# A convolution stage on TensorE: taps for 64 rows and two heads in the two halves of the array

## The chip, the cores and the metric

The kernel runs on one core of a Trainium2 chip. The metric is the device time of one execution in microseconds (us). TensorE (PE, matmuls; PEld, its weight loads), VectorE (DVE), ScalarE (ACT), GpSimd (POOL) and SyncE (SP) each have an instruction queue of their own, and 16 DMA engines serve the DMA queue that SyncE issues to. They meet at semaphores.

## The reference

The input x is 64 batches x 32 heads x 512 positions. Two layers follow each other:

```python
# layer 0: a causal convolution per head, masked by each batch's length
kernel = 2 * real(einsum(Cs, exp(dtA * arange(512))))     # 32 heads x 512 taps
y = irfft(rfft(x * mask, 1024) * rfft(kernel, 1024))[..., :512] + x * mask * D
x = x + y * mask
# layer 1: a gated MLP with one low-rank adapter per batch
gate, up = lora(x @ W_gate.T), lora(x @ W_up.T)           # 1376 wide
x = x + lora((silu(gate) * up) @ W_down.T)
```

All is fp32. The convolution is done as matrix products: for head h, output block k (128 positions) is the sum over d of T_d times input block k-d, where T_d is a 128x128 Toeplitz matrix with the taps 128(d-1)+1 to 128(d+1)-1 in it. D and the residual are added to tap 0.

## The kernel before, in words

**Preparation (0 to 27 us).** VectorE and ScalarE build, for each of four groups of 8 heads, tables from which TensorE makes the taps (`taps`, L965, 8 small matmuls a group). VectorE copies them out of PSUM (L733, L734) and SyncE stores them to a DRAM tensor `kpad`, one row of 128 zeros and 512 taps per head (`store_taps`, L247, semaphore `k_out[group]`).

**Convolution (27 to 78 us).** The 32 heads go in 16 pairs, `PAIRS`. For each pair SyncE loads

- `um` (L258, 256 KB): the pair's input, 128 positions on the partitions, 4 blocks x 64 batches x 2 heads. The positions within a block are reversed, so that the shifted rows below make a Toeplitz matrix;
- `toep` (L253, 512 KB): the shifted taps. Partition r gets, for both heads, 512 taps beginning at r+1 of the padded row, straight from `kpad`. Columns dP to (d+1)P of it are T_d.

Both have `RC` = 4 slots, and the loads of pair p wait until pair p-4 is multiplied (`conv_ps`). TensorE's `conv(pair)` (L969 to L980) waits for the slot's two semaphores and for `x1_ok`, that the PSUM bank has been read. Then for each of the two heads and each d of 0 to 3 it makes one matmul of 128 rows, 128 weight columns and (4-d) x 64 moving columns, all into one PSUM bank: head 0 in its first 256 columns, head 1 in the others. That is 8 matmuls a pair; every fp32 matmul stands in the trace as two records, each with a weight load (LDWEIGHTS), so 16 and 16. Four banks take turns (`ps_c` = `ps_g[0]`, `ps_g[1]`, `ps_u[0]`, `ps_u[1]`). VectorE's `add_conv` (L761) puts the result into `x` where the length mask is set; the last pair is done in two pieces (`select_conv`, L769).

TensorE's order is written out by hand:

```python
taps(0); conv(0); taps(1); conv(1); conv(2); taps(2); conv(3); taps(3)
for pair in range(RC, PAIRS): conv(pair)
```

SyncE's order, too: one in-order queue for all transfers. Before and among the convolution's loads stand the loads of `x` (8 x 512 KB), the gate and up weights (`w_raw`, 12 pieces), and for the first tile of the next stage the adapter tables `a_raw` (4 x 152 KB, after pair 8's taps) and `b_raw` (L311, 4 x 64 KB, each into 16 partitions, after pair 9's). After pair 15's taps come the down weights (`wd_raw`, L236, 6 pieces) and `bd_raw`. `store_taps(2)` and `store_taps(3)` stand behind the taps of pairs 6 and 7; pair 8's taps wait for the landing of the third store.

Beside it ScalarE and GpSimd, and late in the stage VectorE, split the weights into a high and a low part (L440, L404, L776).

**MLP (79 to 543 us).** 16 tiles of 4 batches x 32 heads. For each tile TensorE multiplies x by the gate and up weights (L1024), adds the adapters, and, after the gate, multiplies by the down weights (L1062). The change touches nothing here but how the PSUM tensors `ps_g`, `ps_u` and `ps_x` are declared.

## Time and profile before

| | |
|---|---|
| median of 3 runs | 544.09 us (543.97 to 545.04) |
| the profiled execution | 544.7 us, its span 543.0 |
| mean granted clock of TensorE | 0.997 of 2.4 GHz |
| TensorE busy | 505.7 us (93% of the span), weight loads 459.8 |
| VectorE, ScalarE, GpSimd busy | 344.3, 190.5, 41.5 us |
| chain that ended last | PE 86%, DVE 6%, DMA 5% |
| HBM | 52.89 MB read, 8.47 MB written |

The rows speak of two stages: TensorE is the bound in the MLP stage, and the transfers share the convolution stage with it. In a row, `L978` is the line of the kernel, `ps_g<-um,toep` what is written and read, `128*128` rows and columns of the weights, and `[2.30 <-DMA toep<-kpad]` the idle time before the group and what ended it. A group's duration is from its first start to its last modelled end, so it is longer than the distance to the next group.

### The profile page before, as it was taken

The page shows a single profiled execution, that of the slowest core. Times are in us where ns is not written, and L with a number is a line of the kernel's source. Part 1 is how long each engine was busy: PE and PEld are TensorE (multiplying, and loading weights), DVE is VectorE, ACT ScalarE, POOL GpSimd, SP SyncE. Part 2 cuts the span into 40 slices and gives each one's busy share as a digit, 9 for nine tenths or more (in the row PEclk, how much of TensorE's full clock was granted, in tenths as well). Part 3 has the DMA queues.
Part 4 walks back from the last instruction along what each step waited for, and adds up shares of the span by engine and source line. Part 5 has one row for each costly group of instructions (what it writes and reads, how often), then busy time and mean ns, then how long its engine had stood idle before and what let it go on. Part 6 is the DMA issues. An engine that isn't in the chain of part 4 may idle for free.

```text
span 543.0 us, 10229 instructions
## 1 busy us (share of the span) xinstructions
PE 505.7 (93%) x3045; PEld 459.8 (85%) x3045; DVE 344.3 (63%) x812; ACT 190.5 (35%) x411; POOL 41.5 (8%) x55
## 2 busy tenths in 40 slices
PE   0098889999999999999999999999999999999997
PEld 0097787989898999989898989898989898999986
DVE  7883266757483939383848475766758483939381
ACT  6790007433333333232324232333333333324220
POOL 1006700101000000000000001000001000001000
PEclk9999899999999999999999999999999999999999
DMA  7899993424132323232323323131414132424200
GB/s 278 277 365 388 320 332 68 111 56 111 46 111 48 114 52 114 52 108 57 96 64 95 66 80 82 53 96 49 114 49 109 43 110 52 114 52 114 53 19 21
DMA packets 68403, 61.59 MB, mean 113 GB/s; under 512 B 41634, under 2 KB 50242, under 8 KB 68386
## 3 DMA queue, kind: packets, MB, share of 16 engines
q1 hardware_dynamic: 68386, 61.39, 39.4%
q8 instruction: 8, 0.13, 0.1%
q14 instruction: 9, 0.07, 0.0%
HBM read 52.89 MB, written 8.47 MB: 113 GB/s over the span
## 4 chain that ended last, share of the span: by engine, by line
PE 86%; DVE 6%; DMA 5%; ACT 1%; issue 1%; SPq 0%; DVEq 0%
PE ps_g L1024 21%; PE ps_u L1024 21%; PE ps_db L1062 13%; PE ps_da L1062 13%; PE ps_x L1004 3%; PE ps_g L978 3%; DMA toep<-kpad 2%; PE ps_x L1053 2%; DMA kpad<-k_sb 2%; PE ps_u L978 2%; PE ps_u L1035 2%; PE ps_u L1034 2%; PE ps_g L1034 2%; PE ps_g L1035 2%; PE ps_da L1123 1%
## 5 line engine op out<-in xcount | busy, mean ns | idle before, releaser
L494 ACT CAST b_spl<-b_raw 64x512 fp32r<-64x512 f32 (+1 forms) x96 | 54.7, 572 | 97.1 <-PE ps_u L1035 78.1
L870 DVE STREAM_TRANSPOSE ps_x<-h_act 32x128 f32<-32x128 f32 x240 | 77.4, 323 | 3.8
L1024 PE MATMUL ps_g<-w_hi,x_hi 128*128 128x512 f32 (+1 forms) x192 | 71.2, 371 | 1.4 <-DVE x_lo L935 1.4
L1024 PE MATMUL ps_u<-w_hi,x_lo 128*128 128x512 f32 (+1 forms) x192 | 71.5, 372 | 0.0
L1024 PE MATMUL ps_u<-w_hi,x_hi 128*128 128x512 f32 (+1 forms) x192 | 71.4, 372 | 0.0
L1024 PE MATMUL ps_u<-w_lo,x_hi 128*128 128x512 f32 (+1 forms) x192 | 71.3, 372 | 0.0
L1024 PE MATMUL ps_g<-w_hi,x_lo 128*128 128x512 f32 (+1 forms) x192 | 71.3, 371 | 0.0
L1024 PE MATMUL ps_g<-w_lo,x_hi 128*128 128x512 f32 (+1 forms) x192 | 71.2, 371 | 0.0
L822 DVE TENSOR_TENSOR b_spl<-b_raw,b_spl 64x512 fp32r<-64x512 f32 (+1 forms) x96 | 63.5, 662 | 4.4 <-ACT b_spl L494 0.7
L1062 PE MATMUL ps_da<-wd_hi,ht_hi 128*128 128x288 f32 (+1 forms) x176 | 54.6, 310 | 0.2 <-DVE ht_lo L879 0.2
L1062 PE MATMUL ps_db<-wd_hi,ht_hi 128*128 128x288 f32 (+1 forms) x176 | 53.1, 302 | 0.0
L1062 PE MATMUL ps_db<-wd_hi,ht_lo 128*128 128x288 f32 (+1 forms) x176 | 52.0, 296 | 0.0
L1062 PE MATMUL ps_db<-wd_lo,ht_hi 128*128 128x288 f32 (+1 forms) x176 | 51.9, 295 | 0.0
L1062 PE MATMUL ps_da<-wd_lo,ht_hi 128*128 128x288 f32 (+1 forms) x176 | 51.7, 294 | 0.0
L1062 PE MATMUL ps_da<-wd_hi,ht_lo 128*128 128x288 f32 (+1 forms) x176 | 51.7, 294 | 0.0
L928 DVE TENSOR_TENSOR td_m<-ps_db,amask_t 128x128 f32<-128x128 f32 x16 | 4.7, 292 | 64.8 <-PE ps_db L1062 64.8
L429 POOL COPY xt<-x 128x512 f32 (+1 forms) x15 | 10.0, 667 | 414.3 <-DMA a_raw<-atab 414.3
L1024 PEld LDWEIGHTS ps_g<-w_hi,x_hi 128*128 128x128 f32 x192 | 36.0, 188 | 6.4 <-issue 1.5
L879 DVE TENSOR_TENSOR ht_lo<-ps_x,ht_hi 128x512 fp32r<-128x512 f32 (+1 forms) x48 | 28.9, 603 | 19.5 <-ACT ht_hi L531 18.1
L1024 PEld LDWEIGHTS ps_u<-w_hi,x_lo 128*128 128x128 f32 x192 | 36.0, 188 | 5.9
L1024 PEld LDWEIGHTS ps_u<-w_hi,x_hi 128*128 128x128 f32 x192 | 36.1, 188 | 5.7
L1024 PEld LDWEIGHTS ps_u<-w_lo,x_hi 128*128 128x128 f32 x192 | 36.1, 188 | 5.7
(166 smaller groups left out, 939.2 us busy)
## 6 DMA issues: line engine op xcount, KB each, us to landing
a_raw<-atab SPq DMA_DIRECT2D x64, 152.0 KB, 2.3
toep<-kpad SPq DMA_DIRECT2D x16, 512.0 KB, 7.4
b_raw<-btab SPq DMA_DIRECT2D x128, 64.0 KB, 2.1
um<-xr SPq DMA_DIRECT2D x16, 256.0 KB, 5.6
x<-xT SPq DMA_DIRECT2D x8, 512.0 KB, 6.6
w_raw<-wgu SPq DMA_DIRECT2D x8, 512.0 KB, 9.2
xrow<-x_sq SPq DMA_DIRECT2D x64, 64.0 KB, 2.2
y_sb<-xrow SPq DMA_DIRECT2D x16, 256.0 KB, 2.7
```

The source lines that it names most:

```text
L429: nc.gpsimd.tensor_copy(xt[:, :, :].rearrange("p k (h b) -> p k h b", b=BT), x[:, :, :, bass.ds(t * BT, BT)].rearrange("p h k b -> p k h b ...
L494: nc.scalar.copy(b_spl[0:LR, up, 0:w], b_raw[slot][:, up * w:(up + 1) * w]).then_inc(b_hi, 1)
L822: V.tensor_tensor(b_spl[LR:P, up, 0:w], b_raw[slot][:, up * w:(up + 1) * w], b_spl[0:LR, up, 0:w].bitcast(F32), ALU.subtract).then_inc(b_l ...
L870: ins = V.transpose(into[:, :, tok * Q:(tok + 1) * Q], src[:, :, to * Q:(to + 1) * Q])
L879: V.tensor_tensor(ht_lo[:, f0:f0 + full, :], ps_x[bank][:, 0:full * P].rearrange("p (f t) -> p f t", t=P), ht_hi[:, f0:f0 + full, :].bitca ...
L978: last = T.matmul(ps_c[slot][:, at + d * NB:at + KB * NB], toep[:, slot, h, d * P:(d + 1) * P], v, start=(d == 0), stop=(d == KB - 1))
L1004: ins = T.matmul(ps_x[0][:, 0:P], w, xt[:, kb, :], start=(kb == 0), stop=(kb == KB - 1))
L1024: T.matmul(ps[:, 0:w], xs[:, kb, :], ws[:, kb, col:col + w], start=(kb == 0 and xs is x_hi and ws is w_hi), stop=False)
L1034: T.matmul(ps[:, 0:w], t_hi[:, up, :], b_spl[:, up, 0:w], start=False, stop=False)
L1035: T.matmul(ps[:, 0:w], t_lo[:, up, :], b_spl[:, up, 0:w], start=False, stop=True).then_inc(u_ps if up else g_ps, 1)
L1053: ins = T.transpose(ps_x[bank][0:rows, f * P:(f + 1) * P], h_act[:, s, f * P:f * P + rows], ident[:, :])
L1062: ins = T.matmul(ps[:, 0:c1 - c0], hs[0:rows, f, :], ws[0:rows, f, c0:c1], start=(f == 0 and hs is ht_hi and ws is wd_hi), stop=(bank == 1 ...
```

## The change

Each head's shifted taps are kept on 64 partitions instead of 128, with 576 columns instead of 512: head 0 of a pair on partitions 0 to 63, head 1 on 64 to 127. Shifts of 64 to 127 are then read from the same rows 64 columns further on. Each T_d is multiplied in two steps of 64 rows (`half`), for which the input of a head is laid out on the host as 64 partitions with two halves side by side. The two heads' matmuls alternate, and go to two different PSUM banks. So a pair has 16 matmuls of 64 rows instead of 8 of 128, its taps are loaded by two DMAs of 144 KB instead of one of 512 KB, and three double banks take turns (`RP` = 3) instead of four single ones. One of these is `ps_x`, so pair 2 also waits until the mask that was transposed there has been copied out (`amaskt_ok`).

```diff
--- before.py
+++ after.py
@@ -39,6 +39,9 @@
 DA_W = 288
 DB_W = NL - DA_W
 RC = 4
+RP = 3
+HR = P // 2
+HW = NL + HR
 PAIRS = NH // 2
 PA, PB = 32, 16
 HG = 8
@@ -120,7 +123,7 @@
         with ExitStack() as pa:
             with ExitStack() as pz:
                 zeros = sb(pz, "zeros", [NH, P])
-            toep = sb(pa, "toep", [P, RC, 2, NL])
+            toep = sb(pa, "toep", [P, RC, HW])
             um = sb(pa, "um", [P, RC, 2 * KB * NB])
             lmask = sb(pa, "lmask", [P, KB, NB], I32)
             k_sb = sb(pa, "k_sb", [PA, NG, HG, PB])
@@ -141,13 +144,11 @@
         ht_lo = sb(top, "ht_lo", [P, FB, P], F32R)
 
 
-        ps_g = [top.enter_context(nc.psum_tensor(f"ps_g{i}", [P, 512], F32)) for i in range(2)]
-        ps_u = [top.enter_context(nc.psum_tensor(f"ps_u{i}", [P, 512], F32)) for i in range(2)]
+        ps_c = [top.enter_context(nc.psum_tensor(name, [P, 2, 512], F32)) for name in ("ps_gg", "ps_uu", "ps_xx")]
+        ps_g, ps_u, ps_x = ([both[:, i, :] for i in range(2)] for both in ps_c)
         ps_da = top.enter_context(nc.psum_tensor("ps_da", [P, 512], F32))
         ps_db = top.enter_context(nc.psum_tensor("ps_db", [P, 512], F32))
-        ps_x = [top.enter_context(nc.psum_tensor(f"ps_x{i}", [P, 512], F32)) for i in range(2)]
         ps_k = [ps_da, ps_db]
-        ps_c = [ps_g[0], ps_g[1], ps_u[0], ps_u[1]]
 
 
         prm_in, len_in, idx_in = sem("prm_in"), sem("len_in"), sem("idx_in")
@@ -224,9 +225,9 @@
 
             return bass.AP(tensor=kpad, offset=g * HG * (P + NL) + P, ap=[[PB, PA], [P + NL, HG], [1, PB]])
 
-        def shifted_taps(pair):
-
-            return bass.AP(tensor=kpad, offset=pair * (2 * (P + NL)) + 1, ap=[[1, P], [P + NL, 2], [1, NL]])
+        def shifted_taps(pair, h):
+
+            return bass.AP(tensor=kpad, offset=(2 * pair + h) * (P + NL) + 1, ap=[[1, HR], [1, HW]])
 
         block = top.enter_context(nc.Block())
 
@@ -250,7 +251,8 @@
 
                 sp.wait_ge(k_out[group], 16)
                 wait(sp, conv_ps, pair - RC + 1)
-                sp.dma_start(toep[:, slot, :, :], shifted_taps(pair)).then_inc(toep_in[slot], 16)
+                for h in range(2):
+                    sp.dma_start(toep[h * HR:(h + 1) * HR, slot, :], shifted_taps(pair, h)).then_inc(toep_in[slot], 16)
 
             def load_um(pair, slot, first):
                 if not first:
@@ -760,7 +762,7 @@
                 dve.wait_ge(x_in[2 * pair // HG], 32)
                 V.copy_predicated(x[:, 2 * pair:2 * pair + 2, :, :].rearrange("p h k b -> p h (k b)"),
                                   lmask[:, :, :].rearrange("p k b -> p (k b)").unsqueeze(1).broadcast_to([P, 2, KB * NB]),
-                                  ps_c[pair % RC][:, :].rearrange("p (h n) -> p h n", h=2)).then_inc(x1_ok, 1)
+                                  ps_c[pair % RP][:, :, 0:KB * NB]).then_inc(x1_ok, 1)
 
             def select_conv(pair, b0, b1):
 
@@ -769,7 +771,7 @@
                 return V.copy_predicated(
                     x[:, 2 * pair:2 * pair + 2, :, b0:b1],
                     lmask[:, :, b0:b1].unsqueeze(1).broadcast_to([P, 2, KB, b1 - b0]),
-                    ps_c[pair % RC][:, :].rearrange("p (h k b) -> p h k b", h=2, k=KB)[:, :, :, b0:b1])
+                    ps_c[pair % RP][:, :, 0:KB * NB].rearrange("p h (k b) -> p h k b", k=KB)[:, :, :, b0:b1])
 
             def rem_part(n):
                 dve.wait_ge(w_top, n + 1)
@@ -968,15 +970,19 @@
 
             def conv(pair):
                 slot = pair % RC
-                pe.wait_ge(toep_in[slot], 16 * (pair // RC) + 16)
+                pe.wait_ge(toep_in[slot], 32 * (pair // RC) + 32)
                 pe.wait_ge(um_in[slot], 16 * (pair // RC) + 16)
-                wait(pe, x1_ok, pair - RC + 1)
-                for h in range(2):
-                    at = h * KB * NB
-                    for d in range(KB):
-                        v = um[:, slot, h * KB * NB:h * KB * NB + (KB - d) * NB]
-                        last = T.matmul(ps_c[slot][:, at + d * NB:at + KB * NB], toep[:, slot, h, d * P:(d + 1) * P],
-                                        v, start=(d == 0), stop=(d == KB - 1))
+                wait(pe, x1_ok, pair - RP + 1)
+                if pair == RP - 1:
+                    pe.wait_ge(amaskt_ok, 1)
+                for d in range(KB):
+                    for half in range(2):
+                        at = d * P + (1 - half) * HR
+                        for h in range(2):
+                            rows = slice(h * HR, (h + 1) * HR)
+                            v = um[rows, slot, half * KB * NB:half * KB * NB + (KB - d) * NB]
+                            last = T.matmul(ps_c[pair % RP][:, h, d * NB:KB * NB], toep[rows, slot, at:at + P], v,
+                                            start=(d == 0 and half == 0), stop=(d == KB - 1 and half == 1))
                 last.then_inc(conv_ps, 1)
 
             pe.wait_ge(amaskw_ok, 1)
@@ -1141,7 +1147,8 @@
     xT = np.asarray(x).reshape(NB, NH, KB, P).transpose(3, 1, 2, 0).reshape(P, NH * KB * NB)
 
 
-    xr = xT.reshape(P, NH // 2, 2 * KB * NB)[::-1].transpose(1, 0, 2).reshape(NH // 2 * P, 2 * KB * NB)
+    xr = np.asarray(x).reshape(NB, PAIRS, 2, KB, 2, HR)[..., ::-1].transpose(1, 2, 5, 4, 3, 0)
+    xr = xr.reshape(PAIRS * P, 2 * KB * NB)
 
     def interleave(g, u):
 
```

## Rows read from the trace of the kernel before

**Rows 1.** The page: span, and the span in 40 slices of 13.6 us.

```profile
span 543.0 us, 10229 instructions
...
DMA  7899993424132323232323323131414132424200
...
GB/s 278 277 365 388 320 332 68 111 56 111 46 111 48 114 52 114 52 108 57 96 64 95 66 80 82 53 96 49 114 49 109 43 110 52 114 52 114 53 19 21
```

**Rows 2.** TensorE in order of time: start us, us, engine, line, count, [idle before <-releaser].

```profile
27.25 4.87 PE L978 MATMUL ps_g<-um,toep 128*128 128x256 f32 x16 [7.22 <-DMA toep<-kpad]
...
32.05 0.68 PE L965 MATMUL ps_db<-e 128*32 128x16 f32 x16
...
41.86 2.62 PE L978 MATMUL ps_g<-um,toep 128*128 128x256 f32 x16 [0.42 <-DMA toep<-kpad]
...
45.93 2.62 PE L978 MATMUL ps_g<-um,toep 128*128 128x256 f32 x16 [1.45 <-DMA toep<-kpad]
...
54.63 2.62 PE L978 MATMUL ps_g<-um,toep 128*128 128x256 f32 x16 [0.75 <-DMA toep<-kpad]
...
59.55 4.10 PE L978 MATMUL ps_g<-um,toep 128*128 128x256 f32 x16 [2.30 <-DMA toep<-kpad]
...
63.48 4.98 PE L978 MATMUL ps_u<-um,toep 128*128 128x256 f32 x32
...
73.11 4.98 PE L978 MATMUL ps_u<-um,toep 128*128 128x256 f32 x32
```

**Rows 3.** The same view in narrow windows: starts of the records of one head.

```profile
64.29 0.44 PE L978 MATMUL ps_u<-um,toep 128*128 128x128 f32 x3
...
64.40 0.45 PE L978 MATMUL ps_u<-um,toep 128*128 128x128 f32 x3
...
64.51 0.60 PE L978 MATMUL ps_u<-um,toep 128*128 128x64 f32 x3
...
64.57 0.55 PE L978 MATMUL ps_u<-um,toep 128*128 128x64 f32 x2
...
64.68 0.65 PE L978 MATMUL ps_u<-um,toep 128*128 128x256 f32 x2
```

**Rows 4.** The chain of waits from 39 to 60 us: start us, us, what.

```profile
39.17 8.89 DMA kpad<-k_sb
...
51.62 7.89 DMA toep<-kpad
```

**Rows 5.** Stretches: us; busy us and count for PE, PEld, DVE, ACT, POOL; PEclk, DMA share, GB/s.

```profile
35.00:36.00 1.00, 1.00 (x8) 0.95 (x8) 0.93 (x3) 1.00 (x2) 0.00 (x0) 1.00 0.70 200
...
44.00:48.00 4.00, 2.55 (x18) 2.31 (x17) 0.73 (x1) 0.00 (x0) 4.00 (x3) 1.00 1.06 403
...
56.00:60.00 4.00, 1.70 (x10) 1.51 (x10) 0.73 (x1) 0.00 (x0) 3.68 (x3) 0.90 1.06 259
...
59.50:63.50 4.00, 3.95 (x17) 3.66 (x17) 0.00 (x0) 1.14 (x2) 4.00 (x2) 0.61 1.05 373
```

**Rows 6.** The page's DMA issues: KB each, median us from issue to landing.

```profile
toep<-kpad SPq DMA_DIRECT2D x16, 512.0 KB, 7.4
```

**Rows 7.** SyncE's DMA issues in order of time.

```profile
36.08 0.38 SPq L253 DMA_DIRECT2D toep<-kpad  x1
...
52.19 1.87 SPq L311 DMA_DIRECT2D b_raw<-btab  x4
...
69.34 3.65 SPq L236 DMA_DIRECT2D wd_raw<-wd  x6
```

**Rows 8.** VectorE and TensorE around the stage's hand-overs, in order of time.

```profile
39.06 0.74 DVE L761 COPY_PREDICATED x<-lmask,ps_g 128x512 f32<-128x512 int32 x1
...
73.31 0.74 DVE L761 COPY_PREDICATED x<-lmask,ps_g 128x512 f32<-128x512 int32 x1 [0.91 <-PE ps_g L978]
...
79.46 0.48 PE L1024 MATMUL ps_g<-w_hi,x_hi 128*128 128x512 f32 x1 [1.38 <-DVE x_lo L935]
```

**Rows 9.** ScalarE in order of time: its first casts of the down weights.

```profile
85.75 2.00 ACT L440 CAST wd_hi<-wd_raw 128x1024 fp32r<-128x1024 f32 x2
```

## The prediction

> **What bounds the kernel now.** I read the page's slices first: the DMA engines are busy in the first six slices (0 to 81 us) and mostly idle after them [rows 1]. So the change, which touches only the convolution stage before 80 us, acts where transfers matter. Next comes TensorE in order of time [rows 2]: from 27 to 60 us it works a pair and then waits for that pair's shifted taps, 0.42 us before pair 4, 1.45 before pair 5, 0.75 before pair 8 and 2.30 before pair 9; from pair 9 to pair 15 it runs without a gap. The chain of waits says the same: the store of taps takes 8.89 us to land, and the taps of pair 9 another 7.89 [rows 4], since both stand behind a queue that moves 403 GB/s, full, from 44 to 48 us [rows 5]. In the last seven pairs TensorE itself is the bound: 63.48 to 73.11 us is four pairs, **2.41 us a pair** [rows 2]. Pair 9 alone is slower (59.55 to 63.48, 3.9 us): after the wait the granted clock was at its lower level, 1.2 GHz (0.61 in the mean of 59.5 to 63.5 us, where 1 is 2.4 GHz) [rows 2, 5]. The stage ends near 77.9 us (73.11 and two more pairs), VectorE's last selects follow, and the projections start at 79.46 [rows 8]. They read nothing that the change moves except through this end, so a microsecond on the end of pair 15 is a microsecond on the span.
>
> The profiled execution took 544.7 us for a span of 543.0 and lies 0.6 us above the median of 544.1. I sum against it and subtract 0.6.
>
> **The change, part by part.**
>
> *Bytes.* Per pair the taps shrink from 512 KB to two loads of 144 KB, 288 KB. At the 403 GB/s of a full queue [rows 5] that is 1.30 us before and 0.73 after, 0.57 less. But each new load goes to 64 partitions, and the trace shows what narrow loads do: four 64 KB loads of the B tables, 16 partitions each, are issued from 52.19 us [rows 7] and pass between 56 and 60, where the rate is 259 instead of 403 GB/s with the engines no less busy [rows 5]. Four us at 144 GB/s less is 0.58 MB, or 1.4 us; with the 0.65 us that their 0.26 MB are worth they took about 2.1 us, 126 GB/s. So 16 partitions went at 126 and 128 at 403. No row shows 64. The ends are 403 GB/s (0.57 us gained a pair) and 126 GB/s (2.3 us a pair, 1.0 lost). By equal steps for each doubling, the value nearest to both rows, 64 partitions get 403/1.47 = 273 GB/s, 1.08 us a pair: **0.22 us gained**. Which pairs count? Near 35 us the queue runs dry (share 0.70, 200 GB/s [rows 5]), so what the first four save is lost. From 36.08 us, where the taps of pair 4 are issued [rows 7], it stays full until pair 9 has its taps. Six pairs: 6 x 0.22 = **1.3 us**; full width would give 3.4.
>
> That 64 partitions go slower has a rule beside it. The Trainium skill, "SBUF — State Buffer", section "Door 1: The DMA port swizzle", says that partitions 0 to 63 reach only half of the memory's ports, no more than 32 partitions do, so such a load runs at half bandwidth. By it a pair's taps would take 1.46 us and the sum would be 1.0 us of loss (545.1) instead of 1.3 of gain. In kind the trace agrees, 126 against 403 GB/s for 16 partitions.
>
> *Issues.* SyncE issues two loads a pair instead of one: 16 x 0.38 us more [rows 7]. In the stretch that counts the loads stand in the queue for 7 to 8 us anyway [rows 4, 6], so an issue half a microsecond later lands no later: 0. Were the queue short, each pair would pay 0.4 us. The store of the third tap group is issued three such issues later (about 1.2 us) and lands behind the same bytes: 0 as well. The down weights, issued from 69.34 us [rows 7], are first cast at 85.75 [rows 9]: fewer bytes stand ahead of them, nothing to lose.
>
> *TensorE.* Per pair there were 8 matmuls of 128 rows; now there are 16 of 64 rows, each head in its half, with 256 to 64 columns. Each fp32 matmul is two records, with a weight load each. Within a head, records of 128 columns start 0.11 us apart, so a column costs about 0.83 ns; the two of 64 columns and the one after them start at 64.51, 64.57 and 64.68 [rows 3]: 0.17 us for two records whose columns alone need 0.107. What is left over is the load of 128 weight columns, hidden otherwise; it asks for the same 0.11 (0.107) us a record. If the two halves run beside each other, in loads and in streams, each half has 16 records with the old column counts (2560 columns, 2.13 us, and what the loads add): 2.41 us, the same. If not, the pair costs up to twice. No row here shows two row halves at work. Ends: 2.3 us (the weight loads of 64-column records better hidden) and 4.8 us (one after the other: 8 x (0.22 + 0.16 + 0.11 + 0.11)). I take 2.41, as the matmuls are in separate rows and separate PSUM banks and nothing of one is read by the other. Short records are no limit: the 16 of a tap group took 0.6 us (32.05 us), 0.04 each [rows 2].
>
> *PSUM turns.* Three double banks instead of four single ones. Pair p now waits for the select of pair p-3. A select takes 0.74 us and starts 0.2 us behind its pair [rows 8], while two pairs (4.8 us) lie between; early, the select of pair 1 ends at 39.8 us and pair 4 starts at 41.86 [rows 2, 8]. 0. The extra wait of pair 2 for the mask's copy out of PSUM: VectorE makes that copy third after the second tap group (32.05 + 0.6), each of the three no longer than a select's 0.74, so by 34.9; pair 2 can't start before 32.65 + 2.41 = 35.1 [rows 2, 8]: 0. Selects read the same 512 elements from two banks: 0, at worst 0.1 us at the last pair.
>
> Sum: 544.7 - 1.3 = 543.4 in a profiled run, **542.8** for the median. The wait before pair 9 stays, so its slow clock stays.
>
> **The rivals.**
> 1. *The narrow loads cost nothing.* Then pair 9 comes 3.4 us earlier, the waits nearly close, and the clock may hold, 3.9 - 2.4 = 1.5 us more: 544.1 - 4.9 = 539.2. For it: two loads to opposite halves can overlap. Against it: the B tables, four loads to different partitions, did not. Chance 0.22.
> 2. *Narrow loads at half pace*, 202 GB/s: 1.46 us a pair instead of 1.30, so +0.16 x 6 = +1.0, 545.1. For it: the B tables lost more than half of their rate. Against it: their rows are a quarter as wide. Chance 0.10. (It is the case that the Trainium skill's page "SBUF — State Buffer" describes.)
> 3. *The halves' weight loads run one after the other* (the other side). 32 loads x 0.107 = 3.4 us a pair, more than streaming. Chain: 27.25 + 4.9 (pair 0, as before) + 3 tap groups x 0.62 + 15 x 3.42 = 85.3 against 77.9: +7.4, 551.5. All transfer waits vanish beneath it. It decides from (77.9 - 27.25 - 4.9 - 1.9)/15 = 2.92 us a pair on; below that TensorE's loss fits into the waits it has now. For it: the loads already peek out behind 64 columns [rows 3]. Chance 0.18. A pace between, 2.6 to 3.1 us, gives 543 to 546; chance 0.06.
> 4. *The change doesn't do what it says*: the two heads run in turn, 4.8 us a pair and 9.7 for pair 0: 27.25 + 9.7 + 1.9 + 72 = 110.8, +33, 577. Nothing in the trace speaks against it but that nothing forces it. Chance 0.14.
> 5. *A weight load never hides beneath a matmul of its own rows*: 16 x 0.107 + 2.13 = 3.84 us a pair with the halves beside each other, 6.0 for pair 0, end 92.7, 558.9. Before the change this would be 3.84 as well, and rows 2 show 2.41. Chance 0.03. It is a rule of the Trainium skill, "TensorE: Matmul & The Clock Gate", section "Part 3: Packing small matmuls — row/col tiling"; this case's trace contradicts it for full-height matmuls.
>
> **How the numbers follow.** The forecast (own range 541 to 544.5) has 0.27. A difference under 0.2% (1.1 us) can't be told from no change here, so faster means below 543.0, slower above 545.2. Faster: 0.22 + 0.20 of the forecast + 0.02 of the pace between = 0.44. Same: 0.07 + 0.07 of rival 2 + 0.02 = 0.16. Slower: 0.03 + 0.02 + 0.18 + 0.14 + 0.03 = 0.40. The range reaches from about a microsecond below rival 1 to one above rival 3, 538.0 to 552.5, and leaves out rivals 4 and 5 (0.17).
>
> **What would show it.** Pairs 10 to 15 at 2.41 us from start to start, with 32 records each, say that the halves are beside each other; 3.4, 3.8 or 4.8 name rivals 3, 5 and 4. The taps' rate is read from 22 to 30 us, and the gap before pair 9 from TensorE's order of time: still 1 us with a slow clock by the forecast, near nothing by rival 1, over 3 us by rival 2. The start of the first projection, 79.46 now, should stand near 78.2, and all after it should be as before. The prediction is wrong if that start moves by over 2 us either way, or if the time changes by something else than this start.

## The result, and the profile after

The changed kernel takes 548.34 us (median of 5 runs, 546.33 to 549.67); the kernel before 544.9 on the same chips. The ratio is **1.0063** with a 95% interval of 1.0034 to 1.0091, so it is slower by 1.9 to 5.0 us. I had forecast 542.8, and faster. The median is within the range that I gave, but the direction is wrong.

From the page of the changed kernel (span, DMA share and rate in slices of 13.6 us, the taps' loads):

```profile
span 544.6 us, 10757 instructions
...
DMA  7789993424142423232323323142414142323200
GB/s 283 278 263 295 256 298 80 105 52 113 46 115 53 113 52 113 52 101 64 92 62 92 70 67 94 48 103 52 113 45 110 42 113 52 113 52 113 52 19 20
...
toep<-kpad SPq DMA_DIRECT2D x32, 144.0 KB, 5.4
```

It moves 3.7 MB less from HBM, 49.22 MB instead of 52.89, and the slices from 27 to 81 us show where the gain went. The rates there are 263, 295, 256 and 298 GB/s, where the kernel before had 365, 388, 320 and 332 [rows 1]. The first slices' busy digits are nearly the same. Fewer bytes moved, more slowly.

TensorE in order of time (start us, us, line, count, idle before and its releaser):

```profile
42.51 3.70 PE L984 MATMUL ps_uu<-um,toep 64*128 64x256 f32 x32 [2.42 <-DMA toep<-kpad]
46.18 3.13 PE L984 MATMUL ps_xx<-um,toep 64*128 64x256 f32 x32
...
53.40 4.28 PE L984 MATMUL ps_uu<-um,toep 64*128 64x256 f32 x32 [1.68 <-DMA toep<-kpad]
...
62.12 2.62 PE L984 MATMUL ps_gg<-um,toep 64*128 64x256 f32 x32 [2.04 <-DMA toep<-kpad]
65.07 2.62 PE L984 MATMUL ps_uu<-um,toep 64*128 64x256 f32 x32 [0.32 <-DMA toep<-kpad]
...
77.15 2.57 PE L984 MATMUL ps_gg<-um,toep 64*128 64x256 f32 x32
81.11 0.47 PE L1030 MATMUL ps_gg<-w_hi,x_hi 128*128 128x512 f32 x1 [1.39 <-DVE x_lo L937]
```

Pairs 10 to 15 start 2.42 us apart ((77.15 - 65.07)/5) with 32 records each, as fast as before [rows 2]. So the two heads are multiplied side by side and cost TensorE nothing. But the gaps before the pairs have grown: 2.42 us before pair 4, 1.68 before pair 7, 2.04 before pair 9. Pair 9 starts at 62.12 us, where it was 59.55 before, and the projections at 81.11 instead of 79.46 [rows 2, 8]: 1.65 us. Pair 9 is 2.57 us late, and about 1.0 us of that comes back at once: pair 10 starts 2.95 us behind it, where the kernel before, at the lower clock, took 3.93. The spans differ by 1.6 us (544.6 against 543.0). This profiled run is the fastest of the five (546.33 us); no trace of a slower one is at hand.

Stretches (busy us and count of PE, PEld, DVE, ACT, POOL; then PEclk, DMA share, GB/s):

```profile
44.00:48.00 4.00, 4.00 (x34) 3.62 (x34) 0.74 (x1) 0.00 (x0) 4.00 (x3) 0.59 1.08 271
56.00:60.00 4.00, 4.00 (x50) 3.86 (x46) 0.73 (x1) 0.00 (x0) 0.24 (x1) 0.81 1.07 260
59.50:63.50 4.00, 1.96 (x26) 1.73 (x24) 0.73 (x1) 0.43 (x1) 3.74 (x3) 1.00 1.07 259
```

From 44 to 48 us the queue is as full as before (share 1.08), and moves 271 GB/s instead of 403 [rows 5]. The granted clock is at 1.2 GHz for most of it too, and again from 54 to 58 us, so pairs 4, 5 and 7 take 3.7, 3.0 and 4.1 us; in the kernel before only pair 9 did that among the pairs from 4 on. The lower clock of these three pairs cost nothing in this trace: pair 9, behind them, waits 2.04 us for its taps all the same.

Two earlier stretches, first of the changed kernel (from 24 to 28 us only taps pass, from 34 to 41 mostly x), then the second one in the kernel before:

```profile
24.00:28.00 4.00, 1.80 (x8) 1.53 (x10) 3.79 (x10) 3.56 (x6) 0.00 (x0) 1.00 0.75 236
34.00:41.00 7.00, 6.09 (x96) 5.65 (x92) 5.95 (x17) 6.95 (x10) 0.31 (x1) 1.00 0.85 238
```

```profile
34.00:41.00 7.00, 7.00 (x64) 6.58 (x64) 5.56 (x16) 6.94 (x10) 0.00 (x0) 1.00 1.00 325
```

There the queue is not as full as before (share 0.85 against 1.00), so the rate of narrow loads alone doesn't explain the loss in it.

SyncE's queue in the kernel before, then in the changed one, and its issues of taps (shortest, median, longest ns):

```profile
22.16 1.92 SPq L253 DMA_DIRECT2D toep<-kpad  x4
```

```profile
22.22 5.00 SPq L255 DMA_DIRECT2D toep<-kpad  x8
...
52.55 1.10 SPq L255 DMA_DIRECT2D toep<-kpad  x2
```

```profile
L255 SPq DMA_DIRECT2D toep<-kpad x32: 444/596/633, 22.2 to 71.1; - x32
```

An issue to 64 partitions takes 0.60 us in the median, one to 128 partitions took 0.38 [rows 7]: eight from 22.22 us on take 5.0 us, where four took 1.9. That is 144 KB in 0.63 us, 236 GB/s, just what passes from 24 to 28 us with the engines 0.75 busy: there the issues set the pace. Two theories for the loss come out of this, **narrow loads** (64 partitions are fed at a lower rate) and **issues** (SyncE's queue), and a third one, the **clock**. The experiments were measured on four chips, each beside runs of the kernel before, whose medians were 544.8 to 545.4 us there; I compare by ratio.

### The profile page after: what moved, and what is told of

Same layout as the page of the kernel before. It is cut to its first block, busy times and chain, and to the rows that moved or that the text cites. A ratio compares the mean times of both kernels' runs of the same rounds, so it can differ in the third digit from the quotient of the medians.

```text
span 544.6 us, 10757 instructions
## 1 busy us (share of the span) xinstructions
PE 507.2 (93%) x3301; PEld 461.3 (85%) x3301; DVE 344.8 (63%) x812; ACT 189.8 (35%) x411; POOL 43.3 (8%) x55
## 3 DMA queue, kind: packets, MB, share of 16 engines
q1 hardware_dynamic: 66594, 57.72, 38.7%
HBM read 49.22 MB, written 8.47 MB: 106 GB/s over the span
## 4 chain that ended last, share of the span: by engine, by line
PE 87%; DVE 5%; DMA 4%; SPq 2%; ACT 1%; issue 1%; DVEq 0%
PE ps_gg L1030 21%; PE ps_uu L1030 21%; PE ps_db L1068 13%; PE ps_da L1068 13%; PE ps_xx L1010 3%; PE ps_gg L984 2%; PE ps_xx L1059 2%; DMA toep<-kpad 2%; PE ps_uu L1041 2%; PE ps_uu L1040 2%; PE ps_gg L1040 2%; PE ps_gg L1041 2%; DMA kpad<-k_sb 2%; PE ps_uu L984 1%; PE ps_xx L984 1%
## 5 line engine op out<-in xcount | busy, mean ns | idle before, releaser
L872 DVE STREAM_TRANSPOSE ps_xx<-h_act 32x128 f32<-32x128 f32 x240 | 77.4, 323 | 3.8
L1030 PE MATMUL ps_gg<-w_hi,x_hi 128*128 128x512 f32 (+1 forms) x192 | 71.2, 371 | 1.4 <-DVE x_lo L937 1.4
L1030 PE MATMUL ps_uu<-w_hi,x_lo 128*128 128x512 f32 (+1 forms) x192 | 71.5, 372 | 0.0
L1030 PE MATMUL ps_uu<-w_hi,x_hi 128*128 128x512 f32 (+1 forms) x192 | 71.4, 372 | 0.0
L1030 PE MATMUL ps_uu<-w_lo,x_hi 128*128 128x512 f32 (+1 forms) x192 | 71.3, 372 | 0.0
L1030 PE MATMUL ps_gg<-w_hi,x_lo 128*128 128x512 f32 (+1 forms) x192 | 71.3, 371 | 0.0
L1030 PE MATMUL ps_gg<-w_lo,x_hi 128*128 128x512 f32 (+1 forms) x192 | 71.2, 371 | 0.0
L1068 PE MATMUL ps_da<-wd_hi,ht_hi 128*128 128x288 f32 (+1 forms) x176 | 54.6, 310 | 0.3 <-DVE ht_lo L881 0.3
L1030 PEld LDWEIGHTS ps_gg<-w_hi,x_hi 128*128 128x128 f32 x192 | 36.0, 188 | 6.4 <-issue 1.5
L1030 PEld LDWEIGHTS ps_uu<-w_hi,x_lo 128*128 128x128 f32 x192 | 36.0, 188 | 5.8
L1030 PEld LDWEIGHTS ps_uu<-w_hi,x_hi 128*128 128x128 f32 x192 | 36.1, 188 | 5.7
```

The source lines that it names most:

```text
L872: ins = V.transpose(into[:, :, tok * Q:(tok + 1) * Q], src[:, :, to * Q:(to + 1) * Q])
L1030: T.matmul(ps[:, 0:w], xs[:, kb, :], ws[:, kb, col:col + w], start=(kb == 0 and xs is x_hi and ws is w_hi), stop=False)
L1068: ins = T.matmul(ps[:, 0:c1 - c0], hs[0:rows, f, :], ws[0:rows, f, c0:c1], start=(f == 0 and hs is ht_hi and ws is wd_hi), stop=(bank == 1 ...
```

## The experiments

**The same bytes in one load of full width.** Both halves get their rows from the pair's first head, which leaves the second head's own taps out of the result.

```diff
-            return bass.AP(tensor=kpad, offset=(2 * pair + h) * (P + NL) + 1, ap=[[1, HR], [1, HW]])
+            return bass.AP(tensor=kpad, offset=(2 * pair + h) * (P + NL) + 1, ap=[[1, P], [1, HW]])
...
-                for h in range(2):
-                    sp.dma_start(toep[h * HR:(h + 1) * HR, slot, :], shifted_taps(pair, h)).then_inc(toep_in[slot], 16)
+                sp.dma_start(toep[:, slot, :], shifted_taps(pair, 0)).then_inc(toep_in[slot], 16)
...
```

> The changed kernel with one load of taps a pair, 128 partitions x 576 columns (288 KB, the same bytes as the two loads of 144 KB): both halves take their rows from the pair's first head, so the second head is multiplied with wrong taps; everything else is as in the change. Narrow theory (a load to 64 partitions moves at about half the rate): the taps now move at 400 GB/s, the gaps before pairs 4 to 10 nearly close, 538 to 540 us. Issue theory (SyncE's two issues of 0.6 us a pair are what costs): also one issue, 539 to 541. Packet theory (2304-byte packets are slow in themselves): still 545 to 549.

541.37 us, ratio 0.9919 (0.9894 to 0.9945): 4.4 us faster than before. TensorE in order of time, and a stretch:

```profile
57.77 3.96 PE L983 MATMUL ps_gg<-um,toep 64*128 64x256 f32 x32 [1.94 <-DMA toep<-kpad]
```

```profile
44.00:48.00 4.00, 3.54 (x51) 3.31 (x49) 0.73 (x1) 0.00 (x0) 4.00 (x2) 1.00 1.06 398
```

The queue is back at 398 GB/s with 2304-byte packets, so packets are no cause. Pair 9 starts at 57.77 us. Against the changed kernel (1.0063/0.9919 = 1.0145, 7.9 us) the number of bytes is the same; the width of the loads and the number of issues differ. It was a little slower than the narrow theory's 538 to 540, as the gap before pair 9 stayed (1.94 us), and with it the slow pair 9. In this trace, which is of the slowest of the six executions (543.06 us), pair 9 comes 1.8 us earlier than before, not the 3.4 of full width.

**The kernel before with narrow loads.**

```diff
-                sp.dma_start(toep[:, slot, :, :], shifted_taps(pair)).then_inc(toep_in[slot], 16)
+                for half in range(2):
+                    sp.dma_start(toep[half * (P // 2):(half + 1) * (P // 2), slot, :, :],
+                                 shifted_taps(pair, half)).then_inc(toep_in[slot], 16)
...
```

> The kernel before, its 512 KB of taps a pair loaded as two DMAs of 64 partitions each, the same bytes and packets of 2048 bytes. Narrow theory: 2.4 to 2.6 us of transfer a pair instead of 1.3, 7 us or more over pairs 4 to 9 and the last pairs bound by transfers too: 552 to 562 us. Issue theory: only 0.4 to 0.6 us of issue a pair more, 545 to 547. Clock theory (the loss of the change is only in pairs at the lower clock): no more than 546.

560.87 us, ratio 1.0282 (1.0244 to 1.032). The same two views:

```profile
72.11 4.95 PE L981 MATMUL ps_g<-um,toep 128*128 128x256 f32 x16 [2.80 <-DMA toep<-kpad]
```

```profile
44.00:48.00 4.00, 2.93 (x14) 2.70 (x15) 0.00 (x0) 0.00 (x0) 4.00 (x3) 0.81 1.05 245
```

245 GB/s. Were 256 KB of input at 403 GB/s (0.65 us) and 512 KB of taps at half of that (2.60 us), the mean would be 786,432 bytes in 3.25 us, 242 GB/s. Where taps alone are in the queue, from 26 to 32 us, they pass a little faster than at half pace, at 236 GB/s instead of 201:

```profile
26.00:32.00 6.00, 4.61 (x16) 4.26 (x16) 5.66 (x15) 5.88 (x9) 0.00 (x0) 1.00 1.06 236
```

Pair 9 starts 12.6 us later than before. Ten pairs of 1.3 us give that, and six don't: here the queue doesn't run dry at 35 us (share 1.05 from 34 to 41 us), so the pairs before pair 4 count as well. The time is in the range of the narrow theory (552 to 562) and far above those of the other two: 545 to 547 for the issues, no more than 546 for the clock.

**The kernel before, two loads of full width.** One for each head, so the issues are doubled and nothing else.

```diff
-                sp.dma_start(toep[:, slot, :, :], shifted_taps(pair)).then_inc(toep_in[slot], 16)
+                for h in range(2):
+                    sp.dma_start(toep[:, slot, h, :], shifted_taps(pair, h)).then_inc(toep_in[slot], 16)
...
```

> The kernel before, its taps loaded as two DMAs of 128 partitions, one for each head: the same bytes and packets, two issues instead of one, no narrow load. Narrow theory: no change, 544 to 545 us. Issue theory: as much slower as the change or the halves are, 546 to 548.

545.38 us, ratio 1.0002 (0.9982 to 1.0021). TensorE's pair 9:

```profile
60.44 4.29 PE L979 MATMUL ps_g<-um,toep 128*128 128x256 f32 x16 [2.45 <-DMA toep<-kpad]
```

A second issue of full width costs nothing. These were issues of 0.43 us, though, not of 0.60. Pair 9 starts 0.9 us later than in the trace of before at the same kernel time, so single traces place it no better than that.

**Width, or place?** The 512 KB as three loads: partitions 32 to 95, 0 to 31 and 96 to 127.

```diff
-                sp.dma_start(toep[:, slot, :, :], shifted_taps(pair)).then_inc(toep_in[slot], 16)
+                for r0, r1 in ((32, 96), (0, 32), (96, 128)):
+                    sp.dma_start(toep[r0:r1, slot, :, :], shifted_taps(pair, r0, r1)).then_inc(toep_in[slot], 16)
...
```

> The kernel before, its 512 KB of taps loaded as three DMAs: partitions 32 to 95, 0 to 31, 96 to 127. By place (a load is slow when its partitions lie on one side of 64; one across the middle is not): 0.65 us for the middle and 0.65 for each 128 KB at the side, 1.95 us a pair, half of the loss that halves gave: 550 to 554 us. By number (the rate goes with the count of partitions): 1.3 + 1.3 + 1.3 us or more a pair, twice the loss of halves: 570 to 580. The Trainium skill, page SBUF — State Buffer, section Door 1, describes the first of the two.

554.07 us, ratio 1.0146 (1.0109 to 1.0183), half of the halves' loss (1.5 against 2.8%) with one issue more. TensorE's pair 9:

```profile
66.75 2.62 PE L980 MATMUL ps_g<-um,toep 128*128 128x256 f32 x16 [2.53 <-DMA toep<-kpad]
```

66.75 us is 7.2 us later than before; 10 x 0.65 = 6.5 was the price by place. So it isn't the number of partitions. What the middle load gets can be read late in the stage, where nothing but input and taps is in a full queue:

```profile
76.00:84.00 8.00, 7.26 (x46) 6.53 (x45) 5.00 (x7) 0.00 (x0) 0.00 (x0) 1.00 1.07 270
```

270 GB/s lies between 302 (786,432 bytes in 2.60 us, by place) and 242 (all taps at half pace). So 64 partitions across the middle are fed well above half rate, if not quite at the full one, and 32 or 64 on one side of it near half. The Trainium skill, page "SBUF — State Buffer", section "Door 1: The DMA port swizzle", has this rule (all of 0 to 63 reach the even half of the ports only), and here the runs agree with it.

**Both halves at once, from two queues.** From pair 4 on ScalarE issues the second head's taps.

```diff
+            def load_toep_1(pair):
+                slot = pair % RC
+                act.wait_ge(k_out[pair // RC], 16)
+                act.wait_ge(conv_ps, pair - RC + 1)
+                act.dma_start(toep[HR:P, slot, :], shifted_taps(pair, 1)).then_inc(toep_in[slot], 16)
...
```

> The changed kernel, from pair 4 on the second head's taps are issued by ScalarE on its own DMA queue, so that both halves can be under way at once; SyncE issues only the first head's. Narrow theory: where two narrow loads go to opposite halves at the same time their slowness cancels, 540 to 544 us. If the DMA engines take the two queues in turn in step, no better than the change, 546 to 549. Issue theory: SyncE is relieved of 0.6 us a pair, 543 to 545.

548.28 us, ratio 1.005 (1.0023 to 1.0078), as slow as the change. Pair 9:

```profile
63.03 4.28 PE L994 MATMUL ps_gg<-um,toep 64*128 64x256 f32 x32 [2.97 <-DMA toep<-kpad]
```

SyncE issues one narrow load a pair less, and no gain shows. The two intervals leave room for one of up to some 3 us, so this bounds what the issues cost from pair 4 on and doesn't put it at nothing. Nor did the two queues mend the narrow loads, though loads to opposite halves were under way at the same moment: by its packets of 2304 bytes the first half of pair 4's taps passes from 38.2 to 41.5 us and the second from 38.7 to 41.5, those of pair 8 from 52.1 to 56.1 and 52.6 to 54.6. The full queue stayed at the changed kernel's pace:

```profile
44.00:48.00 4.00, 3.10 (x28) 2.88 (x24) 0.73 (x1) 0.00 (x0) 4.00 (x3) 0.68 1.08 260
```

**TensorE with one half.** Both heads are multiplied from partitions 0 to 63. The second head's values are left out.

```diff
-                            rows = slice(h * HR, (h + 1) * HR)
+                            rows = slice(0, HR)
```

> The changed kernel with both heads multiplied from partitions 0 to 63, in the same half of the array (the second head gets the first one's taps and input, so its values are left out). Side-by-side theory: without the second half the 32 records run one after the other, 4.7 to 4.8 us a pair instead of 2.41, the stage ends near 110 us, 572 to 578 us. If 64-row matmuls overlap for another reason (short records, or both PSUM banks), no change: 546 to 550.

649.05 us (one run). TensorE in order of time, with two pairs of the stage and four matmuls of the projections after it (distances are what counts), and a stretch:

```profile
151.92 9.59 PE L984 MATMUL ps_uu<-um,toep 64*128 64x256 f32 x32
161.31 9.59 PE L984 MATMUL ps_xx<-um,toep 64*128 64x256 f32 x32
...
182.23 0.63 PE L1030 MATMUL ps_gg<-w_lo,x_hi 128*128 128x512 f32 x1
182.66 0.63 PE L1030 MATMUL ps_gg<-w_hi,x_lo 128*128 128x512 f32 x1
...
187.85 0.40 PE L1030 MATMUL ps_uu<-w_lo,x_hi 128*128 128x512 f32 x1
188.08 0.40 PE L1030 MATMUL ps_uu<-w_hi,x_lo 128*128 128x512 f32 x1
```

```profile
150.00:160.00 10.00, 10.00 (x37) 9.25 (x37) 1.50 (x2) 0.00 (x0) 0.00 (x0) 1.00 0.54 187
```

9.39 us a pair, twice the 4.7 that I expected. The other factor of two is the clock. At 182 us the projections' matmuls start 0.43 us apart and at 188 us 0.23. The weight loads of the stage say the same:

```profile
L984 PEld LDWEIGHTS ps_gg<-um,toep x192: 284/333/334, 26.4 to 179.8; 64*128 64x128 f32 x192
```

They take 0.33 us in the median, as in pair 0 of the kernel before (0.34), and never the 0.19 of its later pairs. So TensorE ran at 1.2 GHz through the whole stage, 150 us of nearly gapless work with 64 rows at a time, and rose only at 186 us, in the projections, which use all rows. The granted clock's column shows 1.00 there; where a trace begins, the distance of the records is the better measure. In cycles the pair took 3.9/2 = 1.95 times as long: without the second half nothing overlaps.

**Head after head.** The same matmuls in the two halves, in another order.

```diff
-                for d in range(KB):
-                    for half in range(2):
-                        at = d * P + (1 - half) * HR
-                        for h in range(2):
+                for h in range(2):
+                    for d in range(KB):
+                        for half in range(2):
+                            at = d * P + (1 - half) * HR
```

> The changed kernel with the pair's 16 matmuls in another order: all eight of the first head (partitions 0 to 63), then all eight of the second (64 to 127), instead of in turn. In-order theory (matmuls start in program order, so the halves overlap only where neighbours in the program lie in different halves): nearly no overlap and, as in the run with one half, the lower clock, 9.4 us a pair, 645 to 650 us. If TensorE looks ahead far enough to start the second head early, 2.4 to 3 us a pair, 546 to 560.

629.13 us (one run), below the 645 to 650 of the in-order theory and far above 546 to 560. A pair takes 8.0 us (36.30 to 44.31), at the lower clock again (weight loads of 0.33 us):

```profile
36.30 8.32 PE L984 MATMUL ps_uu<-um,toep 64*128 64x256 f32 x29
44.31 0.79 PE L984 MATMUL ps_xx<-um,toep 64*128 64x256 f32 x1
44.41 0.84 PE L984 MATMUL ps_uu<-um,toep 64*128 64x64 f32 x3
```

So only matmuls near each other in the program overlap: where the half changes, the next head's first record (44.31) starts before the last three of the one before it (44.41 on), and the rest follow one another. Each of the two changes of half in a pair saves 0.69 us ((9.39 - 8.01)/2) against the run with one half. The change's order, the heads in turn, is what keeps TensorE at its pace. (The Trainium skill, "TensorE: Matmul & The Clock Gate", section "Part 3: Packing small matmuls — row/col tiling", says that matmuls start and end strictly in program order; by these records that does not hold for the starts where the half changes.)

**Another order of the loads.** The waits suggested moving loads away from the taps of pairs 4 to 9. In the first try (for both kernels) the last 1 MB of x, `a_raw` and `b_raw` go behind the taps of pairs 9 to 12.

```diff
-                    load_x(3, pair - RC - 2)
...
-                if pair == 2 * RC:
-                    load_a(0, 0, ids0)
-                if pair == 2 * RC + 1:
+                if pair in (2 * RC + 1, 2 * RC + 2):
+                    load_x(3, pair - 2 * RC - 1)
+                if pair == 2 * RC + 3:
+                    load_a(0, 0, ids0)
+                if pair == 2 * RC + 4:
```

> The kernel before with SyncE's order changed: the last two loads of x (2 x 512 KB) go behind the taps of pairs 9 and 10 instead of pairs 6 and 7, a_raw (608 KB) behind pair 11's and b_raw (4 narrow loads of 64 KB) behind pair 12's instead of 8's and 9's. Queue theory (the stage waits only because the queue holds too much ahead of pairs 4 to 9, and narrow loads make that queue slower): 1.6 MB or 4 us less stand ahead of pair 9's taps, the gaps close and the clock holds, 539.5 to 541.5 us. Latency theory (the taps come late because of the store of taps and the landing itself): 543.5 to 545.5, no change.

> The changed kernel with the same reordering of SyncE's loads. Queue theory: the half-wide taps still pass in 1.46 us a pair beside 0.65 for the input, within TensorE's 2.41, so the gaps close here too: 540 to 542.5 us, at most 1 us from the reordered kernel before. If matmuls of 64 rows cost something of their own that the gaps hid: 543 or more, and over 2 us behind it.

546.93 us, ratio 1.0041 (1.0019 to 1.0064), and for the changed kernel 550.36, 1.0089 (1.006 to 1.0118): 2.2 and 1.4 us slower than without it. The kernel before with this order:

```profile
44.38 6.69 PE L979 MATMUL ps_g<-um,toep 128*128 128x256 f32 x32 [2.74 <-DMA toep<-kpad]
...
55.72 4.98 PE L979 MATMUL ps_g<-um,toep 128*128 128x256 f32 x32
...
65.23 2.62 PE L979 MATMUL ps_u<-um,toep 128*128 128x256 f32 x16 [1.67 <-DMA toep<-kpad]
70.24 2.62 PE L979 MATMUL ps_g<-um,toep 128*128 128x256 f32 x16 [2.39 <-DMA toep<-kpad]
```

```profile
48.00:52.00 4.00, 4.00 (x25) 3.75 (x25) 1.47 (x2) 0.00 (x0) 3.50 (x2) 0.88 0.72 231
```

The gaps before pairs 5 to 9 are gone (55.72 is pairs 8 and 9 without one), but the moved loads now delay pairs 11 and 12, by 1.67 and 2.39 us. Also, from 48 to 52 us the queue is no longer full (share 0.72): taps can only be loaded into a free slot, and the x loads had filled that time. Queue theory, as I put it, was wrong for this order. This trace is of one of the slowest executions (549.79 us), and its pair 4 waits 2.74 us where the kernel before waits 0.42, though no load ahead of pair 4's taps was moved: how long that wait is differs from execution to execution.

The changed kernel in this order is 2.6 us behind the kernel before in it (1.0089 against 1.0041), where I had allowed 1, and put more than 2 down to a cost of the 64-row matmuls. Its trace doesn't say that: pairs 6 to 9 start 2.41 us apart (49.05, 51.46, 53.86, 56.27 us), and its gaps, 1.91, 1.35 and 2.28 us, stand before the taps of pairs 10, 11 and 12.

**No second copy of the input.** The convolution's matmuls read x itself, so 4 MB of full-width loads fall away.

```diff
-                pe.wait_ge(um_in[slot], 16 * (pair // RC) + 16)
+                pe.wait_ge(x_in[2 * pair // HG], 32)
...
-                        v = um[:, slot, h * KB * NB:h * KB * NB + (KB - d) * NB]
+                        v = x[:, 2 * pair + h, 0:KB - d, :].rearrange("p k b -> p (k b)")
...
```

> The kernel before without the 16 loads of um (256 KB each, 4 MB in all): the host lays x out with the positions of each block of 128 reversed, the rows and columns of the weights that belong to positions likewise, and the convolution's matmuls read x itself; taps stay on 128 partitions in one load. All of the result is computed. Bytes theory (from pair 4 to 9 the stage is as fast as the queue moves full-width bytes): 0.65 us a pair less, the gaps close, the stage ends 6 to 8 us earlier, 536 to 539.5 us, below both kernels. Slot and latency theory (as the reordering of SyncE's loads suggests, a pair's taps come late because they are issued only when a slot is free and the store has landed): the gaps stay, 542 to 545.

539.84 us, ratio 0.9902 (0.9882 to 0.9922). As built, x is reversed within its blocks and the matmuls' results are not, so they are put over x in the other order of positions. The work is all there, the values are other ones, and it stands for the time only (the expectation says otherwise).

```profile
56.46 2.62 PE L967 MATMUL ps_g<-x,toep 128*128 128x256 f32 x16 [0.30 <-DMA toep<-kpad]
...
68.54 4.98 PE L967 MATMUL ps_u<-x,toep 128*128 128x256 f32 x32
```

Pair 9 waits 0.30 us, and no other pair after pair 0; pairs 14 and 15 start at 68.54 instead of 73.11 [rows 2], 4.6 us earlier, where I had expected the stage's end 6 to 8 us earlier. Bytes of full width, taken out of the queue, do shorten the stage.

**The weights later.** Four pieces of the weights (1.4 MB), which nobody needs before the third chunk, leave the stretch before the taps of pair 4, x takes their place, and they are loaded behind the taps of pairs 11, 12 and 15; the casts and subtractions on two of them move along. All of the result is computed, from the same bytes.

```diff
-            load_piece(2 * KB)
+            load_x(1, 0)
             for pair in range(RC):
                 load_toep(pair, pair, 0)
-            for n in range(2 * KB + 1, NP_GU):
-                load_piece(n)
-            load_x(1, 0)
-            store_taps(1)
             load_x(1, 1)
             load_x(2, 0)
+            load_x(2, 1)
+            store_taps(1)
...
+                if pair in (2 * RC + 3, 2 * RC + 4):
+                    load_piece(pair - 3)
...
```

> The kernel before with another order of the same loads: the last four pieces of the gate and up weights (4 x 352 KB) leave the stretch of 21 to 27 us, where four 512 KB loads of x take their place; two of the pieces go behind the taps of pairs 11 and 12, two behind those of pair 15, and the casts and subtractions on them move with them. So 1.0 MB of x no longer stand in the queue between 34 and 60 us. Bytes theory: pair 9 has its taps 2 to 3 us earlier, the other pairs still within TensorE's pace: 541 to 543 us. If the waits only move to later pairs, as in the first reordering, 544 to 547.

> The changed kernel with that same order of loads. Bytes theory with half-wide loads at half pace (2.1 us a pair for input and taps): again 1 to 3 us later than the kernel before in the same order, 543 to 546 us. If the order mends what the narrow loads cost, within 1 us of it.

The kernel before gets 543.4 us, ratio **0.9971** (0.9953 to 0.9989), faster than both kernels of this study; the changed one 546.49, ratio 1.0029 (1.0011 to 1.0047). First the kernel before in the new order, then the changed one:

```profile
58.53 3.87 PE L980 MATMUL ps_g<-um,toep 128*128 128x256 f32 x16 [2.15 <-DMA toep<-kpad]
...
72.28 4.98 PE L980 MATMUL ps_u<-um,toep 128*128 128x256 f32 x32
78.64 0.48 PE L1026 MATMUL ps_g<-w_hi,x_hi 128*128 128x512 f32 x1 [1.38 <-DVE x_lo L935]
```

```profile
57.69 2.62 PE L986 MATMUL ps_gg<-um,toep 64*128 64x256 f32 x32 [1.51 <-DMA toep<-kpad]
...
70.71 2.62 PE L986 MATMUL ps_uu<-um,toep 64*128 64x256 f32 x32 [0.99 <-DMA toep<-kpad]
...
80.16 0.47 PE L1032 MATMUL ps_gg<-w_hi,x_hi 128*128 128x512 f32 x1 [1.39 <-DVE x_lo L937]
```

Pair 9 comes at 58.53 us, 1.0 us earlier than before, less than the 2 to 3 that I expected, and the projections at 78.64. The changed kernel has pair 9 early, too (57.69), but then waits before four more pairs, as before pair 13 here: with input and taps 2.11 us of transfer a pair leave 0.3 us of TensorE's 2.41 for anything else, where the kernel before has 0.46. It is 1.5 us behind in its projections (80.16), and 0.6% in the ratios (1.0029/0.9971), the same distance as in the old order.

## Why the prediction was wrong

**The step that failed** is *Bytes*, "64 partitions get 403/1.47 = 273 GB/s, 1.08 us a pair: 0.22 us gained". I laid a line by doublings between 16 partitions (126 GB/s) and 128 (403), as if the number of partitions counted. What counts is the side. In a full queue, beside the input, a load that lies wholly on one side of partition 64 is fed at about half rate, 201 GB/s, so a pair's taps take 1.46 us instead of 1.30: longer than the 512 KB did. The runs show it twice. The mix of input and taps in the halved kernel before should pass at 242 GB/s by half pace, and passed at 245. In the changed kernel it should be 557,056 bytes in 0.65 + 1.46 us, 264 GB/s (322 by my 1.08 us), and from 59.5 to 63.5 us it was 259. It isn't exactly a half everywhere: taps alone passed at 236 GB/s. The run in thirds shows that 64 partitions as such are not slow. This was my rival 2, to which I gave 0.10, and its mechanism is the one of the Trainium skill's page "SBUF — State Buffer", which I had named in the prediction. It should have carried the sum: no row spoke against it, and the 0.68 of the full rate that I took for 64 partitions was no measurement.

**Half pace alone doesn't give the size.** Rival 2 counts six pairs (4 to 9), +1.0 us. In the halved kernel ten pairs fit (12.6 us for 10 x 1.3), which would make it +1.6 here. But in the changed kernel's own trace the queue is not full from 34 to 41 us (share 0.85), so ten isn't shown for it. That trace has pair 9 2.57 us late, of which half pace prices 1.0 to 1.6. The rest has a candidate in the issues, which I had put at 0: from 34 to 41 us 238 GB/s pass instead of 325, 0.6 MB less (only 0.26 MB of what passes are taps), while SyncE issues without a pause and is 2.3 us late with the load of x at 42.07 us (39.75 before). No run separates that stretch. ScalarE's queue took half of the taps' issues away in it, but SyncE, held before pair 4's taps until 36.78 us there, was nearly as late (41.67).

The medians differ by 3.4 us (1.9 to 5.0), the traces by 1.65. In the trace of the changed kernel pair 9 ran at the full clock. In the trace with two queues (548.34 us) it ran at the lower one, 4.11 us, and the projections start at 83.14. Whether the slower executions of the changed kernel are of that kind is open: the mean granted clock doesn't order them (0.994 in the fastest, 546.33 us, and 0.997 in one of 548.97).

**What held, and what is only consistent.**
- *TensorE*: 2.42 us a pair with 32 records, as I took it (2.41). Rivals 3, 4 and 5 fall. The one-half run shows what rival 4 would have cost, and more: I had put it at 4.8 us a pair without the lower clock, and it is 9.4.
- *A weight load hides beneath a matmul of its own rows*: the side-by-side halves have 16 records each in 2.41 us, 0.15 us a record. If a load never overlapped its own half, that would be 3.84 us, as in rival 5.
- *PSUM turns*: no wait on a select appears before any pair; the gaps that the trace names all end with taps.
- *Issues*: priced at 0. A second full-width issue costs nothing and moving half of the issues away gains nothing, so while the queue is full, from 44 us on, nothing speaks against 0. Before that it doesn't hold as I argued it: the taps of the first four pairs came at the pace of the issues, and from 34 to 41 us they are the candidate named above. That a narrow issue takes 0.60 instead of 0.38 us I had not foreseen.
- *"The wait before pair 9 stays, so its slow clock stays"*: the wait did, but the clock was up for pair 9 and down for pairs 4, 5 and 7. The forecast of the projections' start, 78.2, was 2.9 us too early in this trace. It moved by 1.65 us, which is within the 2 us that I had set as the sign of being wrong: the sign was too wide for a gain of 1.3.
- *Rival 1* (the narrow loads cost nothing, 539.2): the load of full width shows what it would have been, 4.4 us of gain (3.0 to 5.8 by its interval) against my 4.9. So in the time saving the bytes was worth about what I thought, and narrow loads with their issues took it away and more. By the trace the agreement is partly luck: pair 9 came 1.8 us earlier instead of 3.4, and its clock didn't hold.

## What to carry to other kernels

Nearly halving a tile's bytes by keeping it on half of the partitions gained nothing here, where the queue is full for most of the stage: 64 partitions on one side of the middle were fed at about half the rate (236 GB/s alone, 201 by the mix with input, instead of 403). Look for a layout that spans both sides in every load, or lies across the middle, and ask of every narrow load what it delays behind it. On TensorE, two 64-row products can run beside each other at no cost, if the program gives them in turn; one after the other they cost 1.7 times the cycles (8.0 us at half the clock against 2.41), and here the lower clock on top. And loads that stand behind a filled queue are only worth moving to where no tile waits: moved by three pairs they cost 2 us, moved out of the stretch they gained 1.6.

## What I hadn't expected of the hardware

- With only 64 rows at a time TensorE stayed at 1.2 GHz for 150 us of nearly gapless matmuls (record distances twice as long until 186 us; full-height matmuls had begun at 181.66), and head after head it stayed there too, while the same records side by side run at 2.4 GHz. Each of the two is one run.
- Matmuls of opposite halves can start out of the program's order: 44.31 us for the later one, 44.41 for the earlier, at a change of half.
- An issue of a load to 64 partitions keeps SyncE's queue for 0.60 us in the median where two follow each other, and 0.45 where it stands alone (two queues, from 43 us on); one with more bytes to 128 partitions takes 0.38.
- Loads to opposite halves from two queues, under way at the same time, moved no more than one after the other from one queue: 260 and 271 GB/s from 44 to 48 us.
- The granted clock's column reads 1.00 before the first recorded change, whatever the pace: pair 0 takes 4.87 us at 1.00 [rows 2].
